# Flamingo block on one core: cross keys turned in a score bank, weight means one step sooner, another order for the step without a tile

## The chip, the cores and the metric

One core of a Trainium2 chip runs the whole kernel. The metric is device time in microseconds (us), median of repeated runs. The engines are TensorE (PE; its weight loads PEld), VectorE (DVE), ScalarE (ACT), GpSimd (POOL) and SyncE (SP), which issues most transfers. Each works through its own list of instructions in order and waits only at semaphores.

## What is computed

```python
x = x + tanh(g_xattn) * xattn(layernorm(x), ctx)      # x: 8 x 112 x 512, ctx: 8 x 375 x 512
x = x + tanh(g_ffn) * moe_ffn(layernorm(x))           # 8 experts, top 2

# xattn: 16 query heads, 8 key/value heads of 128
q  = ln(fp8_linear(h, wq));  k = ln(fp8_linear(h, wk));  v = fp8_linear(h, wv)
qx = ln(fp8_linear(h, wqx)); kx, vx = split(ctx @ w_kv_x.T); kx = ln(kx)
cat = concat(softmax(q k / sqrt(128)) v, softmax(qx kx / sqrt(128)) vx)
out = fp8_roundtrip(cat / smooth) @ wproj.T
```

## The kernel before

Four stages follow each other: the inputs are normalised and rounded, then attention, the output projection, and the experts. The change touches the attention alone.

**Steps.** The 16 query heads fall into four groups `g` of four, the batch has eight sequences `u`. A step takes a pair: `s = (g, u)`, whose projections are computed, and `t`, the one before it, whose attention is computed. So the two halves of a step are independent, and the engines interleave them. The 896 token rows make seven tiles of 128, though each sequence has 112 rows: steps 0 to 6 of a group have a tile of q, qx and k to project, **step 7 has none** and projects only values and the context (`has_tile`, `last_step`). `passes` writes steps 1 to 7 and 0 of the next group as the body of a loop run three times (groups 0 to 2), and those of group 3 once more without a loop. Time follows `u`: step 1 is the first of a body, and the step 0 that ends it does the first projections of the next group.

**Within a step.** On TensorE `project` 0 to 5 make q, qx, k with v, and three chunks of the context, each in a bank of `p_proj` in turn. `turn` 0 to 4 transpose the normalised q, qx, k and the two heads of the context keys (`nkx`) of `t` in the banks of `p_tr`, one after the other (0, 1, 0, 1, 0). `score_self` and `score_cross` 0 to 3 fill `p_self` and the two banks of `p_cross`; `turn_self` and `turn_cross` 0 to 3 transpose the probabilities in `p_tr`; `outputs` 0 and 1 multiply them with the values in `p_out`. `bank_free` holds the waits for the banks.

ScalarE takes projections out of PSUM and squares them (`take`), copies turned heads (`turned`), and makes the exponentials. VectorE sums the squares (`sums`), GpSimd makes `rs` of them (`rstd`), VectorE scales (`scale`). VectorE also finds the maxima, normalises the probabilities (`norm_self`, `norm_cross`), copies their transposes (`take_self`, `take_cross`), multiplies the output (`smoothed`), rounds it in five operations (`rounded`) and copies the next inputs (`inputs`). The order on every engine is written out by hand in its `step` and `last_step`.

Projections run in fp32 as sums of products of parts: weights and context are split into `hi` (ScalarE: `w_high`, `c_high`) and `lo` (VectorE: `w_low`; GpSimd: `c_low`). `c_low` of a chunk stands ahead of `rstd` of the same number in `last_step` on GpSimd: `c_low` 1, `rstd` 3, `c_low` 2, `rstd` 4, `rstd` 5.

**Weights of the next group.** 4 MB are fetched in step 1. For each of four blocks `k`, `weights.means` (L139, L142) sums the columns of each head on VectorE, and `weights.centre` (L158 to L163) subtracts the mean on ScalarE in three parts: in steps 2 to 5. `w_high` and `w_low` for queries (`change == "queries"`) stand in step 6, for keys and values (`"keys"`) in step 7, for the rest (`"new"`) in step 0.

## Time and profile before

| | us |
|---|---|
| three runs | 1277.56, 1278.98, 1281.84 (median 1278.98) |
| the profiled execution | 1275.52 |
| its span, first to last instruction | 1273.8 |
| TensorE busy, matmuls | 1120.3 (88%) |
| VectorE busy | 845.5 (66%) |
| ScalarE busy | 704.5 (55%) |
| GpSimd busy | 476.2 (37%) |
| granted TensorE clock, mean share of full speed | 0.951 |

The attention takes about the first 900 us of the span. In rows in order of time, the first number is the start and the second the duration in us; a bracket at the end holds how long the engine stood idle ahead of the row and which instruction ended that. A matmul's duration overlaps with the next one's; their pace is read from the starts.

### The profile page before, as it was taken

How to read it: one execution, taken by the hardware profiler on the slowest of the kernel's cores; microseconds unless marked ns; L12 is line 12 of the kernel's file. 1: busy time of each engine (PE TensorE's matmuls, PEld its weight loads, DVE VectorE, ACT ScalarE, POOL GpSimd, SP SyncE). 2: the span in 40 equal slices, each digit the busy share in tenths (PEclk: the TensorE clock that was granted, in tenths of full speed). 3: DMA queues.
4: the chain of work that ended last, by engine and by line, in shares of the span. 5: the costliest groups of instructions: out<-in, count | busy, mean ns of one | idle time of the engine just before them, and what ended most of it. 6: DMA issues, size and time to landing. Idle time of an engine off the chain costs nothing. (4 is left out here: it accounts for less than half of the span.)

```text
span 1273.8 us, 21650 instructions
## 1 busy us (share of the span) xinstructions
PE 1120.3 (88%) x5656; PEld 904.7 (71%) x5656; DVE 845.5 (66%) x1704; ACT 704.5 (55%) x1794; POOL 476.2 (37%) x584
## 2 busy tenths in 40 slices
PE   1099999899999979999988999997799949999996
PEld 1078777677777857877776788885588737777785
DVE  7967777786778768788777877876543665746100
ACT  7966777654777844676765646654111413434442
POOL 3074435343454423443443434432000132655432
PEclk9589999999999989999989999999899958999999
DMA  5041111114111111411111311110446066666220
GB/s 191 23 168 47 32 33 48 40 41 166 38 51 40 33 32 34 180 49 33 33 51 35 133 32 48 41 40 15 150 155 240 25 228 201 190 202 183 55 42 1
DMA packets 51736, 107.61 MB, mean 84 GB/s; under 512 B 5984, under 2 KB 26464, under 8 KB 49568
## 3 DMA queue, kind: packets, MB, share of 16 engines
q1 hardware_dynamic: 46912, 97.00, 23.2%
q0 software_dynamic: 4704, 9.18, 3.2%
q8 instruction: 55, 0.90, 0.3%
q14 instruction: 65, 0.53, 0.1%
HBM read 91.48 MB, written 16.52 MB: 85 GB/s over the span
## 5 line engine op out<-in xcount | busy, mean ns | idle before, releaser
L604 POOL TENSOR_TENSOR c_lo<-c_raw,c_hi 128x500 fp32r<-128x500 f32 x96 | 135.5, 1412 | 189.9 <-ACT c_hi L655 189.8
L806 PE MATMUL p_proj<-w_hi,xqs 128*128 128x512 f32 (+2 forms) x464 | 159.1, 362 | 51.2 <-DVE w_lo L529 41.0
L833 PE MATMUL p_proj<-w_hi,c_hi 128*125 128x512 f32 x384 | 167.9, 437 | 0.0
L591 POOL TENSOR_TENSOR va<-ss,epst 125x2 f32<-125x2 f32 (+1 forms) x180 | 61.6, 342 | 263.5 <-DVE ss L1000 263.5
L598 POOL TENSOR_TENSOR rs<-va,mhalf 125x2 f32<-125x2 f32 (+1 forms) x180 | 148.4, 825 | 15.6 <-POOL va L591 2.9
L833 PE MATMUL p_proj<-w_lo,c_hi 128*125 128x512 f32 x384 | 153.8, 401 | 0.0
L833 PE MATMUL p_proj<-w_hi,c_lo 128*125 128x512 f32 x384 | 153.7, 400 | 0.0
L806 PE MATMUL p_proj<-w_lo,xqs 128*128 128x512 f32 (+2 forms) x464 | 149.3, 341 | 0.0
L1000 DVE TENSOR_REDUCE ss<-sq 125x2 f32<-125x256 f32 (+1 forms) x180 | 89.7, 499 | 82.4 <-ACT sq L665 76.1
L806 PEld LDWEIGHTS p_proj<-w_hi,xqs 128*128 128x128 f32 (+1 forms) x464 | 87.2, 188 | 66.3 <-issue 45.0
L726 ACT ACTIVATE pcross<-p_cross,nmax 112x375 f32<-112x375 f32 x128 | 73.2, 577 | 78.2 <-DVE nmax L1029 77.3
L874 PE MATMUL p_cross<-kxT,qxT 128*112 128x375 f32 x256 | 97.4, 482 | 0.0
L1284 PE MATMUL p_acc<-p_hi,p_catr 128*128 128x512 f32 x224 | 88.5, 395 | 9.1 <-DVE p_lo L1329 9.1
L806 PEld LDWEIGHTS p_proj<-w_lo,xqs 128*128 128x128 f32 (+1 forms) x464 | 87.5, 189 | 8.5
L1284 PE MATMUL p_acc<-p_lo,p_catr 128*128 128x512 f32 x224 | 88.1, 393 | 0.0
L833 PEld LDWEIGHTS p_proj<-w_hi,c_hi 128*125 128x125 f32 x384 | 73.1, 190 | 20.0 <-issue 1.7
L158 ACT ACTIVATE shared<-shared,w_mean,wsc 128x128 f32<-128x128 f32 x160 | 65.9, 486 | 37.3 <-DVE w_mean L142 37.3
L833 PEld LDWEIGHTS p_proj<-w_hi,c_lo 128*125 128x125 f32 x384 | 72.7, 189 | 18.5
L833 PEld LDWEIGHTS p_proj<-w_lo,c_hi 128*125 128x125 f32 x384 | 73.0, 190 | 17.9 <-issue 0.3
L665 ACT ACTIVATE sq<-p_proj 125x256 f32<-125x256 f32 (+1 forms) x180 | 84.7, 470 | 0.0
L901 PE MATMUL p_out<-pcrossT,valx 125*128 125x224 f32 x384 | 84.3, 356 | 0.0
L1052 DVE TENSOR_TENSOR yb<-p_out,smg 128x448 bf16<-128x448 f32 x64 | 39.7, 621 | 61.8 <-PE p_out L901 61.8
(234 smaller groups left out, 2726.7 us busy)
## 6 DMA issues: line engine op xcount, KB each, us to landing
c_raw<-in_ctxT SPq DMA_DIRECT2D x96, 250.0 KB, 2.6
shared<-in_w_in SPq DMA_DIRECT2D x16, 1024.0 KB, 9.5
shared<-in_wproj SPq DMA_DIRECT2D x32, 256.0 KB, 2.8
raw_g<-in_Wg SPq DMA_DIRECT2D x8, 1024.0 KB, 6.7
raw_u<-in_Wu SPq DMA_DIRECT2D x8, 1024.0 KB, 5.9
raw_d<-in_Wd SPq DMA_DIRECT2D x8, 1024.0 KB, 5.5
cat_scratch<-cat SPq DMA_DIRECT2D x32, 224.0 KB, 2.0
shared<-cat_scratch SPq DMA_DIRECT2D x2, 1792.0 KB, 8.4
```

The costliest lines, as they stand in the source:

```text
L158: act.activation(cols, cols, ACT.Identity, bias=mean, scale=self.wsc[:, n, block_k])
L591: pool.tensor_tensor(va[0:rows, lo:hi], ss[0:rows, lo:hi], epst[0:rows, lo:hi], ALU.add).then_inc(va_done, 1)
L598: pool.tensor_tensor(rs[0:rows, lo:hi], va[0:rows, lo:hi], mhalf[0:rows, lo:hi], ALU.pow).then_inc(rs_done, 1)
L604: pool.tensor_tensor(flat(c_lo[:, k, :, :]), flat(c_raw[:, k, :, :]), flat(c_hi[:, k, :, :]).bitcast(F32), ALU.subtract).then_inc(cl_done, 1)
L665: act.activation(sq[0:rows, j % 2, 0:n], p_proj[0:rows, j % 2, 0:n], ACT.Square, scale=float(HD) ** -0.5).then_inc(pj_done, 1)
L726: act.activation(pcross[0:T, h, :], p_cross[0:T, h % 2, 0:TC], ACT.Exp, bias=nmax[0:T, 4 + h:5 + h], accum_out=lsum[0:T, 4 + h:5 + h]).the ...
L806: m = pe.matmul(out, xqs[:, n, k, 0:rows], (w_hi, w_lo)[i % 2][:, k, lo:lo + w], start=(i == 0), stop=(i == 2 * KB - 1))
L833: m = pe.matmul(bank[0:CT, :], a[:, ch, k, :], w[:, k, CKX:CV], start=(i == 0), stop=(i == 3 * KB - 1))
L874: pe.matmul(p_cross[0:T, h % 2, 0:TC], qxT[:, t[1] % 2, h, :], kxT[:, h // HPG, :], start=True, stop=True).then_inc(sx_rdy, 1)
L901: m = pe.matmul(p_out[:, HPG * T:2 * HPG * T], valx[0:CT, par, k, g * P:(g + 1) * P], flat(pcrossT[0:CT, k, HPG * g:HPG * (g + 1), :]), st ...
L1000: v.tensor_reduce(ss[0:rows, lo:hi], sq[0:rows, j % 2, 0:(hi - lo) * HD].rearrange("p (h d) -> p h d", d=HD), AX, ALU.add).then_inc(rd_don ...
L1284: m = pe.matmul(acc[:, j, :], catr[:, n % 2, j * P:(j + 1) * P], w[:, n % 2, :], start=(first and part == 0), stop=(last and part == 1), s ...
```

## The change

1. `turn_bank`: the first head of the context keys is turned in bank 1 of `p_cross`, the second in bank 1 of `p_tr`. The transposes of the probabilities change banks in turn; the waits of `bank_free` follow.
2. `means` of block `k` moves from step `k + 2`, ahead of `sums` 3, to step `k + 1`, behind `sums` 5. `centre` stays in steps 2 to 5, its third part ahead of `take` 5 instead of behind. `take` 3 comes ahead of `exp_cross` 2 and 3 on ScalarE.
3. `inputs` moves behind `norm_cross` 2 and 3.
4. `w_low` of the queries moves behind `scale` 5; `w_high` of the keys moves from step 6 to step 7.
5. `last_step` gets another order on TensorE, ScalarE and VectorE.

```diff
@@ -524,6 +524,10 @@
+    def turn_bank(n):
+        return p_cross[:, 1, :] if n == 3 else p_tr[:, {0: 0, 1: 1, 2: 0, 4: 1}[n], :]
     def split_low(eng, n):
@@ -699,11 +703,11 @@
             if n >= 3:
-                act.activation(kxT[:, n - 3, :], p_tr[:, n % 2, 0:TC], ACT.Identity, bias=b,
+                act.activation(kxT[:, n - 3, :], turn_bank(n)[:, 0:TC], ACT.Identity, bias=b,
                                scale=w).then_inc(t_done, 1)
...
             heads = (4, 4, 2)[n]
-            src = p_tr[:, n % 2, 0:heads * P].rearrange("p (h t) -> p h t", t=P)
+            src = turn_bank(n)[:, 0:heads * P].rearrange("p (h t) -> p h t", t=P)
             dst, u = (qT, qxT, kT)[n], t[1]
@@ -732,8 +736,9 @@
             turned(t, 2)
+            c_high(s, 1)
+            if change == "keys": w_high(g, 2, change)
             turned(t, 3)
-            c_high(s, 1)
             take(s, 3)
@@ -766,17 +771,16 @@
             if A: c_high(s, 2)
+            if A: take(s, 3)
             if Q: exp_cross(t, 2)
             if Q: exp_cross(t, 3)
-            if A: take(s, 3)
             if k is not None: weights.centre(act, g, k, 0)
...
             if k is not None: weights.centre(act, g, k, 1)
+            if k is not None: weights.centre(act, g, k, 2)
             if change == "queries": w_high(g, 1, change)
             if A: take(s, 5)
-            if k is not None: weights.centre(act, g, k, 2)
-            if change == "queries": w_high(g, 2, change)
             if A and s[1] == TJ - 1: c_high((s[0], B - 1), 0)
@@ -837,13 +841,15 @@
             if n < 2:
-                pe.wait_ge(pt_done, 5 * lin(t) + 4 + n)
-            elif n < 5 and not has_tile(t):
-                pe.wait_ge(pt_done, 5 * lin(t) + 4 + n % 2)
-            elif n < 7:
-                pe.wait_ge(t_done, td_no(t, n - 2))
+                pe.wait_ge(pt_done, 5 * lin(t) + 5 - n)
+            elif n == 3:
+                pe.wait_ge(ex_done, 4 * lin(t) + 4)
+            elif n >= 7:
+                pe.wait_ge(pt_done, 5 * (lin(t) + 1) + n - 6)
+            elif n < 6 and not has_tile(t):
+                pe.wait_ge(pt_done, 5 * lin(t) + n)
             else:
-                pe.wait_ge(pt_done, 5 * (lin(t) + 1) + n - 6)
+                pe.wait_ge(t_done, td_no(t, {2: 0, 4: 1, 5: 2, 6: 4}[n]))
@@ -852,10 +858,10 @@
                 for h in range((4, 4, 2)[n]):
-                    m = pe.transpose(p_tr[:, n % 2, h * P:(h + 1) * P], src[:, h * P:(h + 1) * P], ident[:, :])
+                    m = pe.transpose(turn_bank(n)[:, h * P:(h + 1) * P], src[:, h * P:(h + 1) * P], ident[:, :])
             else:
                 for k in range(NC):
-                    m = pe.transpose(p_tr[:, n % 2, k * CT:(k + 1) * CT],
+                    m = pe.transpose(turn_bank(n)[:, k * CT:(k + 1) * CT],
                                      nkx[0:CT, k, (n - 3) * P:(n - 2) * P], ident[0:CT, 0:CT])
@@ -878,14 +884,14 @@
             for h in range(HP):
-                m = pe.transpose(p_tr[0:T, 1, h * T:(h + 1) * T], pself[0:T, h, :], ident[0:T, 0:T])
+                m = pe.transpose(p_tr[0:T, 0, h * T:(h + 1) * T], pself[0:T, h, :], ident[0:T, 0:T])
             m.then_inc(tr_rdy, 1)
...
             for k in range(NC):
-                m = pe.transpose(p_tr[0:CT, h % 2, k * T:(k + 1) * T], pcross[0:T, h, k * CT:(k + 1) * CT],
+                m = pe.transpose(p_tr[0:CT, 1 - h % 2, k * T:(k + 1) * T], pcross[0:T, h, k * CT:(k + 1) * CT],
                                  ident[0:T, 0:T])
@@ -909,8 +915,8 @@
             turn(t, 2)
+            project(s, 3)
             turn(t, 3)
-            project(s, 3)
             score_self(t)
@@ -922,9 +928,9 @@
             project(s, 5)
-            outputs(t, 0)
             turn_cross(t, 2)
             turn_cross(t, 3)
+            outputs(t, 0)
             outputs(t, 1)
@@ -1039,13 +1045,13 @@
             v.wait_ge(ou_rdy, 2 * lin(t) + 2)
-            v.tensor_copy(flat(pselfT[0:T, :, :]), p_tr[0:T, 1, 0:HP * T]).then_inc(pt_done, 1)
+            v.tensor_copy(flat(pselfT[0:T, :, :]), p_tr[0:T, 0, 0:HP * T]).then_inc(pt_done, 1)
...
             v.tensor_copy(pcrossT[0:CT, :, h, :],
-                          p_tr[0:CT, h % 2, 0:NC * T].rearrange("p (k t) -> p k t", k=NC)).then_inc(pt_done, 1)
+                          p_tr[0:CT, 1 - h % 2, 0:NC * T].rearrange("p (k t) -> p k t", k=NC)).then_inc(pt_done, 1)
@@ -1072,31 +1078,31 @@
             if change == "keys": w_low(g, 1)
-            sums(s, 3)
             max_self(t)
-            scale(s, 3)
             max_cross(t, 0)
...
             norm_cross(t, 1)
+            sums(s, 3)
             take_self(t)
-            sums(s, 4)
             take_cross(t, 0)
             max_cross(t, 2)
-            scale(s, 4)
+            scale(s, 3)
             take_cross(t, 1)
             max_cross(t, 3)
-            if change == "keys": inputs((s[0] + 1, 0))
+            sums(s, 4)
             norm_cross(t, 2)
             norm_cross(t, 3)
-            if change == "keys": w_low(g, 2)
-            smoothed(t, 0)
+            if change == "keys": inputs((s[0] + 1, 0))
+            scale(s, 4)
             take_cross(t, 2)
             take_cross(t, 3)
+            smoothed(t, 0)
             sums(s, 5)
...
             scale(s, 5)
+            if change == "keys": w_low(g, 2)
             rounded(t)
@@ -1123,10 +1129,9 @@
             if A: scale(s, 2)
-            if A: inputs((s[0], s[1] + 1))
             if Q: norm_cross(t, 2)
             if Q: norm_cross(t, 3)
-            if k is not None: weights.means(v, g, k)
+            if A: inputs((s[0], s[1] + 1))
             if A: sums(s, 3)
@@ -1135,9 +1140,10 @@
             if A: scale(s, 4)
+            if A: sums(s, 5)
+            if change is None and g is not None and s[1] <= KB: weights.means(v, g, s[1] - 1)
+            if A: scale(s, 5)
             if change == "queries": w_low(g, 0)
-            if A: sums(s, 5)
-            if A: scale(s, 5)
             if Q: rounded(t)
```

VectorE in a centring step, before: step 2 of a group (`w_mean` is the tile of means, `shared` the weights, `ss` the sums of squares).

```order
L1036 TENSOR_SCALAR pcross<-pcross,linv 112x375
L136 ISA
L137 ISA
L139 TENSOR_REDUCE w_mean<-shared 128x12
L142 TENSOR_TENSOR w_mean<-w_mean,wmul 128x12
L995 REGISTER_ALU
L1000 TENSOR_REDUCE ss<-sq 125x2
L1051 ISA
L1052 TENSOR_TENSOR yb<-p_out,smg 128x448
L1045 REGISTER_ALU
L1047 COPY pcrossT<-p_tr 125x3x112
```

The same in the change, where it stands in step 1.

```order
L1006 TENSOR_REDUCE ss<-sq 125x2
L136 ISA
L137 ISA
L139 TENSOR_REDUCE w_mean<-shared 128x12
L142 TENSOR_TENSOR w_mean<-w_mean,wmul 128x12
L1012 REGISTER_ALU
L1015 TENSOR_TENSOR nkx<-nkx,rs 125x256
L1066 TENSOR_SCALAR yb<-yb 128x896
```

The two operations on `w_mean` leave the place ahead of the third chunk's sum and `pcrossT`, and stand between the last `ss` and the last scaling of `nkx`.

VectorE at the end of step 6 and the start of step 7, before (`w_lo` 128x4x512 is the queries' part, `yb` the output being rounded).

```order
L1052 TENSOR_TENSOR yb<-p_out,smg 128x448
L1006 REGISTER_ALU
L1009 TENSOR_TENSOR nkx<-nkx,rs 125x256
L529 TENSOR_TENSOR w_lo<-shared,w_hi 128x4x512
L995 REGISTER_ALU
L1000 TENSOR_REDUCE ss<-sq 125x2
L1006 REGISTER_ALU
L1009 TENSOR_TENSOR nkx<-nkx,rs 125x256
L1060 TENSOR_SCALAR yb<-yb 128x896
```

And in the change.

```order
L1058 TENSOR_TENSOR yb<-p_out,smg 128x448
L1012 REGISTER_ALU
L1015 TENSOR_TENSOR nkx<-nkx,rs 125x256
L1001 REGISTER_ALU
L1006 TENSOR_REDUCE ss<-sq 125x2
L1012 REGISTER_ALU
L1015 TENSOR_TENSOR nkx<-nkx,rs 125x256
L533 TENSOR_TENSOR w_lo<-shared,w_hi 128x4x512
L1066 TENSOR_SCALAR yb<-yb 128x896
```

`ss` and `nkx` of the last chunk change places with `w_lo`.

TensorE at the end of step 7, behind project 5, before.

```order
L898 MATMUL p_out<-pselfT,val 128x224
L901 MATMUL p_out<-pcrossT,valx 128x224 x3
L885 REGISTER_ALU
L846 REGISTER_ALU
L888 MATMUL p_tr<-ident,pcross 125x112 x3
L885 REGISTER_ALU
L888 MATMUL p_tr<-ident,pcross 125x112 x3
L895 REGISTER_ALU
L897 REGISTER_ALU
L898 MATMUL p_out<-pselfT,val 128x224
```

And in the change.

```order
L894 MATMUL p_tr<-ident,pcross 125x112 x3
L891 REGISTER_ALU
L848 REGISTER_ALU
L894 MATMUL p_tr<-ident,pcross 125x112 x3
L903 REGISTER_ALU
L904 MATMUL p_out<-pselfT,val 128x224
L907 MATMUL p_out<-pcrossT,valx 128x224 x3
L901 REGISTER_ALU
L903 REGISTER_ALU
L904 MATMUL p_out<-pselfT,val 128x224
```

Both transposes of `pcross` stand ahead of both `outputs` (`p_out`) now.

## Rows read from the trace of the kernel before

**Rows 1.** TensorE in order of time: turn 0 at the steps' starts (start us, us, engine, line, operation)
```profile
235.42 0.60 PE L855 MATMUL p_tr<-ident,nq 128*128 128x128 f32 x4
...
294.00 0.60 PE L855 MATMUL p_tr<-ident,nq 128*128 128x128 f32 x4
...
319.69 0.49 PE L855 MATMUL p_tr<-ident,nq 128*128 128x128 f32 x3
...
444.71 0.60 PE L855 MATMUL p_tr<-ident,nq 128*128 128x128 f32 x4
...
506.70 0.60 PE L855 MATMUL p_tr<-ident,nq 128*128 128x128 f32 x4
...
656.75 0.60 PE L855 MATMUL p_tr<-ident,nq 128*128 128x128 f32 x4
...
715.26 0.60 PE L855 MATMUL p_tr<-ident,nq 128*128 128x128 f32 x4
...
739.67 0.60 PE L855 MATMUL p_tr<-ident,nq 128*128 128x128 f32 x4
...
859.81 0.60 PE L855 MATMUL p_tr<-ident,nq 128*128 128x128 f32 x4
```

**Rows 2.** In order of time: waits in the centring steps 4 and 5 of group 1
```profile
374.35 0.38 PE L806 MATMUL p_proj<-w_hi,xqs 128*128 128x256 f32 x1 [0.43 <-ACT sq L665]
...
414.55 1.75 DVE L139 TENSOR_REDUCE w_mean<-shared 128x12 f32<-128x1536 f32 x1
...
416.62 1.65 ACT L158 ACTIVATE shared<-shared,w_mean,wsc 128x128 f32<-128x128 f32 x4 [3.10 <-DVE w_mean L142]
...
418.42 0.64 PE L898 MATMUL p_out<-pselfT,val 112*128 112x224 f32 x2 [0.34 <-DVE pcrossT L1047]
```

**Rows 3.** TensorE in order of time: step 7 of group 1
```profile
451.07 0.88 PE L858 MATMUL p_tr<-ident,nkx 125*128 125x125 f32 x3 [3.88 <-DVE nkx L1009]
...
456.82 0.95 PE L867 MATMUL p_self<-kT,qT 128*112 128x112 f32 x8
...
464.00 0.60 PE L881 MATMUL p_tr<-ident,pself 112*112 112x112 f32 x4 [1.87 <-DVE pself L1023]
...
474.78 1.11 PE L898 MATMUL p_out<-pselfT,val 112*128 112x224 f32 x2 [1.99 <-DVE pcrossT L1047]
```

**Rows 4.** Step 7 by stretch: us, busy PE, PEld, DVE, ACT, POOL, clock, DMA share, GB/s
```profile
451.00:453.00 2.00, 1.93 (x6) 1.68 (x7) 1.77 (x5) 1.01 (x2) 0.00 (x0) 0.50 0.00 0
```

**Rows 5.** In order of time: ends of step 7, and step 0, groups 1 and 2
```profile
472.07 1.22 DVE L529 TENSOR_TENSOR w_lo<-shared,w_hi 128x1024 fp32r<-128x1024 f32 x1
...
491.03 0.60 PE L881 MATMUL p_tr<-ident,pself 112*112 112x112 f32 x4 [0.59 <-DVE pself L1023]
...
688.08 0.56 PE L806 MATMUL p_proj<-w_hi,xqs 128*128 128x512 f32 x1
...
701.02 0.59 PE L881 MATMUL p_tr<-ident,pself 112*112 112x112 f32 x4 [1.26 <-DVE pself L1023]
```

**Rows 6.** In order of time: keys scaled and turned in group 3
```profile
813.64 0.42 DVE L1009 TENSOR_TENSOR nkx<-nkx,rs 125x256 f32<-125x256 f32 x1 [1.08 <-POOL rs L598]
...
815.89 0.48 PE L858 MATMUL p_tr<-ident,nkx 125*128 125x125 f32 x3
```

**Rows 7.** VectorE in order of time: step 7 of group 1
```profile
445.79 2.28 DVE L529 TENSOR_TENSOR w_lo<-shared,w_hi 128x2048 fp32r<-128x2048 f32 x1
...
449.48 1.45 DVE L1009 TENSOR_TENSOR nkx<-nkx,rs 125x256 f32<-125x256 f32 x1 [1.08 <-POOL rs L598]
...
453.43 3.34 DVE L529 TENSOR_TENSOR w_lo<-shared,w_hi 128x2048 fp32r<-128x2048 f32 x1
...
460.70 0.61 DVE L1015 TENSOR_REDUCE nmax<-p_self 112x4 f32<-112x448 f32 x1
```

**Rows 8.** GpSimd in order of time: step 7 of group 1
```profile
449.42 1.24 POOL L604 TENSOR_TENSOR c_lo<-c_raw,c_hi 128x500 fp32r<-128x500 f32 x1
```

**Rows 9.** TensorE in order of time: step 7 of group 3
```profile
874.29 0.59 PE L881 MATMUL p_tr<-ident,pself 112*112 112x112 f32 x4 [1.92 <-DVE pself L1023]
```

## The prediction

> **What bounds the kernel now.** I read the TensorE rows of the attention in order of time first, since the transposes of the query heads (turn 0) mark every step 1 to 7 of a group. From turn 0 of step 2 to turn 0 of step 7, five periods, it takes 125.0 us in group 1, and 120.1 us in group 3, where no weights are centred [rows 1]. (The last period is some 2 us short, as step 7 has no project 0.) So 4.9 us per group hang on the centring, 14.6 us in three groups. From turn 0 of step 7 to turn 0 of the next step 1 (step 7 and step 0) it takes 58.6, 62.0 and 58.5 us [rows 1]. TensorE is the bound nearly everywhere else in the attention: it waits only where a row shows a bracket.
>
> In a centring step two short waits stand on TensorE: project 2 waits 0.43 us for ScalarE's squares, and the second `outputs` waits 0.34 us for `pcrossT` [rows 2]. Both have one source. VectorE's sum over the weight tile (1.75 us) stands ahead of the copies of `pcrossT`, and ScalarE's centring waits 3.10 us for it, so ScalarE is late into the next step [rows 2]. Records of pipelined matmuls hide part of such waits, which is why I price them by the periods.
>
> In step 7 TensorE stands still 3.88 us ahead of turn 3, runs then at a granted clock of 0.50 (the 1.2 GHz level) and reaches the self scores only at 456.82; it waits 1.87 us for `pself` and 1.99 us for `pcrossT` [rows 3, 4]. Step 0 adds 0.59 us in group 1 and 1.26 us in group 2 [rows 5].
>
> **Means one step sooner, centring ahead of take 5.** The operations and their sizes stay; 12 sums of 1.75 us, each with a multiplication, move behind `sums` 5 and ahead of `scale` 5. Removed: the 2.0 us ahead of the `pcrossT` copies, and ScalarE's 3.10 us wait, since the means are a step old. The first two centring parts (1.65 us each) fit into the stretch in which ScalarE waited 3.10 us [rows 2], and the third comes ahead of take 5 instead of ahead of the next step's turns. If every step came down to group 3's, this would be the whole 14.6 us. Added: 2.0 us ahead of `scale` 5, where VectorE waits 1.08 us for `rs` anyway; so the keys are scaled 0.9 us later. In group 3 they are ready at 814.06 and turn 3 starts at 815.89, 1.8 us later [rows 6]. 0.9 us of cover is left, so I cost it at nothing. The sum now also reads the weights at the end of step 1; they are asked for at the step's start, and whether they have landed in time is a small rival. Bounds: 14.6 us, and below, if half of the waits stay, 7.3 us. I take **14 us**.
>
> **Keys turned in a score bank.** `kx` head 0 goes to `p_cross` bank 1, where it waits for the last exponentials of the step before, long done; head 1 goes to bank 1 of `p_tr`. No row shows TensorE waiting for these banks, so the edit by itself is worth nothing. Inputs behind the cross normalisation: 1.5 us of casts change place with work that TensorE needs only after project 5. Nothing either, in ordinary steps. Nor for `take` 3 ahead of the last two cross exponentials: project 3 is done by then, and ScalarE waits there for VectorE's maxima; its cover gone, it would delay the exponentials by the take's own length, which only the transposes behind project 4 would feel.
>
> **Step 7, group 1, followed through.** Before, `w_lo` of the queries (2.28 us) stood ahead of `sums` 5 [rows 7]. Now the sum follows `scale` 4 directly. That brings everything behind it 2.2 us forward: POOL's `c_lo` of chunk 0 from 449.42 to 447.2, done 448.5 [rows 8]. TensorE does project 3 ahead of turn 3 now. It is free at 447.2 (3.88 us before 451.07) and waits 1.3 us for `c_lo`. Project 3 took 5.2 us at half the clock [rows 3, 4], so 2.6 at least at full clock; with the weight loads I take 2.9. Turn 3 adds 0.4, the self scores start at 451.8 instead of 456.82: 5.0 us sooner.
>
> But VectorE isn't there yet. `scale` 5 runs beside `c_lo` as before (1.45 us) and ends at 448.7. Behind it stand `w_lo` of the queries, the rounding (450.93 to 453.43, 2.5 us) and the next `w_lo`, 2.28 us each alone, 3.34 us beside a `c_lo` [rows 7]. With one of each this ends at 448.7 + 3.34 + 2.6 + 2.28 = 456.9. Only then comes the maximum of the self scores, which started at 460.70 [rows 7]. `sums` 3 and `scale` 3 are out of this chain, so `pself` is turned 3.2 us after it: 460.1 instead of 464.00, 3.9 us sooner. TensorE's work from the self scores to there is 5.3 us (456.82 to 464.00 less 1.87), so it is free at 457.1 and waits 3.0 us. **The stall moves from the scaled keys to VectorE's `w_lo` chain.** With 2.28 us for both `w_lo` it would be 2.0 us.
>
> Here the two orders of VectorE and POOL matter. `scale` 5 started 0.06 us behind a `c_lo` of 1.24 us and took 1.45 us instead of the 0.42 of group 3; the second `w_lo` took 3.34 us and not 2.28 [rows 6 to 8]. The Trainium skill ("SBUF — State Buffer", Who interferes with whom) says that such a pair takes turns at one port pair and that the later one blocks until the first is done. By that rule `w_lo`, which starts at 448.7 right before `c_lo` of chunk 1, would keep its 2.28 us and POOL would pay, and the forecast would be 3 us lower.
>
> From `pself` on: `sums` 3 stands behind the second cross normalisation, 1.0 us after `pself` is turned. POOL needs its statistics (0.9 us) ahead of `c_lo` of chunk 2 (1.25 us), so project 5 can start 3.6 us after `pself` is turned. Project 5 takes 2.9, the last two cross transposes 0.8, `outputs` 0 1.45. Then `outputs` 1 must wait for `smoothed` 0, since both use `p_out`: 0.65 us, new. After 1.45 us more project 0 starts: 10.85 us after `pself` is turned. In group 1 `outputs` 1 alone began 10.8 us after it (464.00 to 474.78) [rows 3]. `w_lo` of the keys (1.22 us) is out of this stretch [rows 5], and stands ahead of the rounding now: step 0's VectorE chain, on which TensorE waited, is 1.2 us longer. From project 0 to the next `pself` it was 12.9 us in group 2 (688.08 to 701.02) [rows 5]; now 12.95 + 1.2 = 14.15.
>
> The sum from turn 0 of step 7 to the next `pself`: 15.4 + 10.85 + 14.15 = 40.4 us, 121.2 in three groups. From there to turn 0 of step 1 nothing changes: 14.2 us in group 2 (701.02 to 715.26) and 15.7 in group 1 (491.03 to 506.70), which I take for group 0 too: 45.6 [rows 1, 5]. That makes 166.8, against 58.6 + 62.0 + 58.5 = 179.1: 12.3 us less. A wait of 3.88 us brought half clock [rows 3, 4]; the new one of 3.0 us may too. It cost 2.6 us at project 3; here part of it lies under POOL's late `c_lo`, so up to 2 us per group: 6.3 us is the lower bound. With two short `w_lo` each group is 1 us sooner: 15.3 us is the upper. I take **10 us**, below the middle, since the new wait is nearer to the one of 3.88 us.
>
> In group 3 there is no `w_lo`, so `pself` is ready for TensorE when it comes: turn 0 at 859.81, `c_lo` at +3.75 as before, project 3 to +6.65, and 5.3 + 0.4 us of work: +12.4 instead of +14.48 [rows 1, 9]. The rest is as above. **2.2 us.** The last step without a projection keeps its order.
>
> **Sum.** 14 + 10 + 2.2 = 26.2 us. The profiled execution took 1275.5 us, 3.5 below the median of 1279.0 that the forecast is for. 1279.0 − 26.2 = **1253 us**. Everything behind the attention starts sooner by the same amount.
>
> **Rivals.**
> *The last step returns nothing:* half clock after the new 3.0 us wait, project 5 behind POOL, and the longer chain of step 0 take back what project 3 gains. For it: three new waits on one path. Against: project 3 no longer stands behind a 3.88 us stall. 1279 − 16 = 1263. Chance 0.12.
> *Centring doesn't pay:* ScalarE stays late, because centring part 2 ahead of take 5 delays the squares of projection 5. Against it: its wait of 3.10 us is given back ahead of them [rows 2]. 1279 − 12 = 1267. Chance 0.05.
> *Both return nothing, stalls only change names:* 1279. Chance 0.03.
> *Slower:* the means ahead of `scale` 5 hold up turn 3. Place: the end of steps 1 to 4, 12 times. It begins to cost beyond the 0.9 us of cover. Up to 2.1 us beyond that it only eats the 26 us that the rest brings, and from there the kernel is slower. At 2 us it may also bring half clock, some 2.6 us each time as at project 3: 12 × 4.6 = 55 us, so 1253 + 55 = 1308. It needs a `scale` 5 that is 2.9 us later than now rather than 0.9, as through weights that haven't landed. Chance 0.04.
>
> **Numbers.** Forecast 0.76 at 1253, with its own range of 1245 to 1259 (the two bounds of step 7, and 1 us of each other term). The range reaches down to 1244 for the port rule and to 1264 to take in the first rival. Less than 0.3% (3.8 us) can't be told from no change: faster 0.93, same 0.03, slower 0.04.
>
> **What would show it.** Right: the five periods of turn 0 near 120.5 us in groups 0 to 2; no wait of ScalarE for the means; self scores of step 7 some 7.1 us after its turn 0; a wait for `pself` of 2 to 3 us in step 7 of groups 0 to 2 and none in group 3; a longer wait than 0.59 us in step 0. Wrong: TensorE waiting for `nkx` in steps 2 to 5, the five periods still at 125 us, or a long stretch at clock 0.50 in the second half of step 7.

## The result: 1247.7 us, 31.7 us less

| | before | after |
|---|---|---|
| median of four runs, us | 1279.34 (1277.56 to 1281.84) | 1247.68 (1244.3 to 1250.32) |
| the profiled execution | 1275.52 | 1250.32 |
| its span | 1273.8 | 1248.6 |

The ratio is 0.975, with a 95% interval of 0.9721 to 0.9779. The forecast was 1253 us, a sum of 26.2 us. The profiled execution of the changed kernel is the slowest of its four, and that of before lies below all four of its runs, so the two profiled times differ by 25.2 us and the medians by 31.7. Up to turn 0 of the last step 7 the traces differ by 30.5 us (859.81 against 829.28). What lies behind that took 414.0 us before and 419.3 after; a second execution of the kernel before, below, took 417.4 us there. Nearly all of it is the projection and the experts, whose code is the same. From the first matmul of the projection to the end the kernel before took 367.0 us with 49.5 us at half clock, its second execution 370.4 us with 56.4, and the changed kernel 371.3 us with 57.3. I compare the attention by traces, and whole kernels by medians.

The profile after, by busy time of the engines, from the page:

```profile
PE 1105.4 (89%) x5656; PEld 903.2 (72%) x5656; DVE 841.9 (67%) x1704; ACT 705.0 (56%) x1794; POOL 487.5 (39%) x584
```

Turn 0 at the steps' starts, TensorE in order of time, the changed kernel, groups 1 to 3 (line numbers behind the edit are 4 to 6 higher):

```profile
311.81 0.60 PE L861 MATMUL p_tr<-ident,nq 128*128 128x128 f32 x4
...
430.83 0.60 PE L861 MATMUL p_tr<-ident,nq 128*128 128x128 f32 x4
...
486.73 0.60 PE L861 MATMUL p_tr<-ident,nq 128*128 128x128 f32 x4
...
630.46 0.60 PE L861 MATMUL p_tr<-ident,nq 128*128 128x128 f32 x4
...
685.60 0.60 PE L861 MATMUL p_tr<-ident,nq 128*128 128x128 f32 x4
...
709.86 0.60 PE L861 MATMUL p_tr<-ident,nq 128*128 128x128 f32 x4
...
829.28 0.60 PE L861 MATMUL p_tr<-ident,nq 128*128 128x128 f32 x4
```

Against [rows 1], the five periods of group 1 fell from 125.0 to 119.0 us. That is 1.1 us below the 120.1 that I took for the floor, and group 3, which has no weights to centre, fell too: from 120.1 to 119.4. Steps 7 and 0 fell from 62.0 to 55.9 in group 1 and from 58.5 to 55.1 in group 2, but in group 0 only from 58.6 to 58.2.

The waits of [rows 2] are gone. Steps 4 and 5 of group 1, VectorE, ScalarE and TensorE in order of time; the sum over the weight tile runs behind `sums` 5 and ScalarE waits for none of it:

```profile
383.84 1.75 DVE L139 TENSOR_REDUCE w_mean<-shared 128x12 f32<-128x1536 f32 x1
...
400.29 1.64 ACT L158 ACTIVATE shared<-shared,w_mean,wsc 128x128 f32<-128x128 f32 x4
...
412.13 0.39 PE L810 MATMUL p_proj<-w_hi,xqs 128*128 128x256 f32 x1 [0.15 <-ACT sq L669]
```

Step 7 of group 1, TensorE, the answer to [rows 3, 5]:

```profile
434.72 0.47 PE L837 MATMUL p_proj<-w_hi,c_hi 128*125 128x512 f32 x1 [1.68 <-POOL c_lo L608]
...
437.91 0.95 PE L873 MATMUL p_self<-kT,qT 128*112 128x112 f32 x8
...
445.98 0.59 PE L887 MATMUL p_tr<-ident,pself 112*112 112x112 f32 x4 [2.46 <-DVE pself L1029]
...
449.70 0.47 PE L837 MATMUL p_proj<-w_hi,c_hi 128*125 128x512 f32 x1 [0.60 <-POOL c_lo L608]
...
455.65 0.65 PE L904 MATMUL p_out<-pselfT,val 112*128 112x224 f32 x2 [0.72 <-DVE yb L1058]
...
457.11 0.56 PE L810 MATMUL p_proj<-w_hi,xqs 128*128 128x512 f32 x1
...
464.26 0.34 PE L810 MATMUL p_proj<-w_hi,xqs 128*112 128x256 f32 x1 [1.81 <-DVE w_lo L533]
...
471.55 0.60 PE L887 MATMUL p_tr<-ident,pself 112*112 112x112 f32 x4 [0.94 <-DVE pself L1029]
```

One stall of 3.88 us has become a chain of small ones: 1.68 for POOL's `c_lo`, 2.46 for VectorE's `pself`, then 0.60, 0.72, 1.81 and 0.94.

### The profile page after: what moved, and what is told of

The parts are those of the page before. It is cut to its first block and busy times, and to the rows that moved or that the text cites. A ratio compares the mean times of both kernels' runs of the same rounds, so it can differ in the third digit from the quotient of the medians.

```text
span 1248.6 us, 21647 instructions
## 1 busy us (share of the span) xinstructions
PE 1105.4 (89%) x5656; PEld 903.2 (72%) x5656; DVE 841.9 (67%) x1704; ACT 705.0 (56%) x1794; POOL 487.5 (39%) x584
## 5 line engine op out<-in xcount | busy, mean ns | idle before, releaser
L608 POOL TENSOR_TENSOR c_lo<-c_raw,c_hi 128x500 fp32r<-128x500 f32 x96 | 143.3, 1493 | 158.0 <-ACT c_hi L659 157.8
L602 POOL TENSOR_TENSOR rs<-va,mhalf 125x2 f32<-125x2 f32 (+1 forms) x180 | 154.6, 859 | 15.6 <-POOL va L595 2.9
L595 POOL TENSOR_TENSOR va<-ss,epst 125x2 f32<-125x2 f32 (+1 forms) x180 | 59.9, 333 | 251.8 <-DVE ss L1006 251.7
L810 PEld LDWEIGHTS p_proj<-w_hi,xqs 128*128 128x128 f32 (+1 forms) x464 | 86.7, 187 | 70.3 <-issue 52.6
L1006 DVE TENSOR_REDUCE ss<-sq 125x2 f32<-125x256 f32 (+1 forms) x180 | 89.3, 497 | 46.3 <-ACT sq L669 43.4
L730 ACT ACTIVATE pcross<-p_cross,nmax 112x375 f32<-112x375 f32 x128 | 73.2, 579 | 53.7 <-DVE nmax L1035 50.6
L880 PE MATMUL p_cross<-kxT,qxT 128*112 128x375 f32 x256 | 100.9, 497 | 0.1
L692 ACT ACTIVATE nkx<-p_proj 125x256 f32<-125x256 f32 x96 | 37.8, 394 | 73.3 <-PE p_proj L837 65.0
```

What stands on the lines that cost most here:

```text
L595: pool.tensor_tensor(va[0:rows, lo:hi], ss[0:rows, lo:hi], epst[0:rows, lo:hi], ALU.add).then_inc(va_done, 1)
L602: pool.tensor_tensor(rs[0:rows, lo:hi], va[0:rows, lo:hi], mhalf[0:rows, lo:hi], ALU.pow).then_inc(rs_done, 1)
L608: pool.tensor_tensor(flat(c_lo[:, k, :, :]), flat(c_raw[:, k, :, :]), flat(c_hi[:, k, :, :]).bitcast(F32), ALU.subtract).then_inc(cl_done, 1)
L730: act.activation(pcross[0:T, h, :], p_cross[0:T, h % 2, 0:TC], ACT.Exp, bias=nmax[0:T, 4 + h:5 + h], accum_out=lsum[0:T, 4 + h:5 + h]).the ...
L810: m = pe.matmul(out, xqs[:, n, k, 0:rows], (w_hi, w_lo)[i % 2][:, k, lo:lo + w], start=(i == 0), stop=(i == 2 * KB - 1))
L880: pe.matmul(p_cross[0:T, h % 2, 0:TC], qxT[:, t[1] % 2, h, :], kxT[:, h // HPG, :], start=True, stop=True).then_inc(sx_rdy, 1)
```

## The experiments

All kernels ran with their own runs of the kernel before (medians 1279.2, 1279.5 and 1278.2 us in the three sets). The last four columns are worked out from the traces. "Attention" goes from turn 0 of the first group's step 1 to turn 0 of the last group's step 7. "Half clock" is how long the granted clock stood at 0.50, the 1.2 GHz level, between turn 0 of step 7 and the next turn 0, from windows of 1 us.

| kernel | median, us | less than before | attention | five periods, g0 / g1 / g2 / g3 | steps 7 and 0, g0 / g1 / g2 | half clock there |
|---|---|---|---|---|---|---|
| before | 1279.3 | | 774.3 | 125.0 / 125.0 / 125.0 / 120.1 | 58.6 / 62.0 / 58.5 | 6.8 / 13.6 / 6.8 |
| e9 before again | 1277.9 | | 772.9 | 124.9 / 124.9 / 124.9 / 120.1 | 59.7 / 59.7 / 58.5 | 6.8 / 6.8 / 6.8 |
| changed | 1247.7 | 31.7 | 743.6 | 119.1 / 119.0 / 119.1 / 119.4 | 58.2 / 55.9 / 55.1 | 10.2 / 0 / 3.4 |
| e1 inputs | 1271.3 | 7.9 | 769.4 | 125.1 / 125.1 / 125.1 / 119.4 | 59.9 / 58.8 / 58.0 | 6.8 / 3.4 / 6.8 |
| e2 means, centring | 1262.0 | 17.2 | 756.1 | 120.0 / 120.2 / 120.2 / 120.0 | 59.0 / 58.7 / 57.8 | 6.8 / 3.4 / 3.4 |
| e5 means alone | 1262.8 | 16.7 | 756.9 | 120.1 / 120.0 / 120.1 / 120.0 | 59.2 / 59.7 / 58.4 | 3.4 / 6.8 / 6.8 |
| e3 last step | 1268.2 | 11.0 | 763.3 | 124.9 / 124.9 / 124.9 / 120.1 | 56.9 / 56.9 / 55.1 | 3.4 / 6.8 / 3.4 |
| e4 banks as before | 1248.5 | 30.7 | 742.1 | 119.1 / 119.1 / 119.0 / 119.4 | 56.1 / 56.9 / 54.7 | 3.4 / 3.4 / 3.4 |
| e10 inputs as before | 1250.5 | 27.7 | 747.3 | 120.0 / 120.1 / 120.1 / 120.0 | 55.9 / 55.8 / 55.0 | 3.4 / 3.4 / 3.4 |
| e6 `c_low` | 1247.6 | 31.9 | 743.6 | 119.1 / 119.1 / 119.1 / 119.5 | 56.1 / 57.1 / 55.9 | 3.4 / 6.8 / 10.2 |
| e7 `w_low` | 1240.8 | 38.7 | 734.9 | 119.1 / 119.1 / 119.0 / 119.5 | 54.3 / 54.0 / 52.5 | 0 / 0 / 0 |
| e12 (e6 and e7) | 1237.9 | 40.3 | 733.9 | 119.1 / 119.1 / 119.1 / 119.4 | 53.7 / 53.6 / 52.6 | 0 / 0 / 3.4 |
| e8 (e12 and two more) | 1231.3 | 48.2 | 729.7 | 119.1 / 119.1 / 119.1 / 119.5 | 52.7 / 52.2 / 50.5 | 3.4 / 0 / 0 |
| e11 `w_low` 1 on POOL | 1237.0 | 41.2 | 736.6 | 119.0 / 119.1 / 119.1 / 119.4 | 55.0 / 54.4 / 53.1 | 3.4 / 3.4 / 3.4 |

### e2 and e5: the means

```diff
             if Q: norm_cross(t, 3)
-            if k is not None: weights.means(v, g, k)
...
             if A: sums(s, 5)
+            if change is None and g is not None and s[1] <= KB: weights.means(v, g, s[1] - 1)
```

e2 also has centring part 2 ahead of `take` 5; e5 is this edit alone.

> The kernel before, with the means one step sooner (behind sums 5 of steps 1 to 4) and the third centring part ahead of take 5; inputs, banks and the last step as before. My prediction: the five periods from turn 0 of step 2 to turn 0 of step 7 fall from 125.0 to 120.1 us, so 14 us less, 1265 us (bounds 7.3 and 14.6 less). The rival by which centring part 2 ahead of take 5 holds up ScalarE: no gain, periods at 125 us, 1279 us. The rival by which the means hold up scale 5: TensorE waits for nkx in steps 2 to 5, over 1279 us.

> The kernel before, with the means one step sooner and nothing else: the third centring part stays behind take 5. If the means ahead of the pcrossT copies were the whole cause of the 4.9 us per group, the periods fall to 120.1 us and the time by 14 us, to 1265 us. If the third centring part ahead of the next step's turns costs as much as ScalarE's lateness did, half of it stays: periods near 122.5 us, 1272 us. If the means ahead of scale 5 hold up turn 3, TensorE waits for nkx and the time is over 1279 us.

e2: ratio 0.9867 (0.9845 to 0.9888), 17.2 us less. e5: 0.9867 (0.985 to 0.9883), 16.7 us less. Turn 0 of steps 2 and 7 of group 1 in e2:

```profile
314.62 0.60 PE L855 MATMUL p_tr<-ident,nq 128*128 128x128 f32 x4
...
434.79 0.60 PE L855 MATMUL p_tr<-ident,nq 128*128 128x128 f32 x4
```

That is 120.2 us, and in three groups the five periods give back 14.7 us (375.1 less 360.4), the whole of the term. TensorE's waits for `pcrossT` are gone in steps 2 to 5, and its waits of 0.43 us at project 2 fell to 0.16 us at most, so the place of the sum ahead of these copies was the cause. The place of centring part 2 is worth nothing: e5, without it, has the same periods. The rival by which it costs something, and the one by which the means hold up turn 3, both fall.

### e1 and e10: the casts of the next inputs

```diff
-            if A: inputs((s[0], s[1] + 1))
             if Q: norm_cross(t, 2)
             if Q: norm_cross(t, 3)
+            if A: inputs((s[0], s[1] + 1))
```

e1 is this edit alone; e10 is the changed kernel without it.

> The kernel before, with one edit: in the steps with a tile the casts of the next inputs stand behind the normalisation of cross heads 2 and 3. My prediction costed this at nothing: 1279 us, ordinary steps of group 3 still 24.42 us apart. The other theory, from the trace of the changed kernel: the ordinary steps there are 24.16 to 24.26 us apart, because the last two normalised cross heads are ready sooner for their transposes. If this edit alone brings that, 0.17 us in each of some 28 steps is 5 us: 1274 us, and the transposes of cross heads 2 and 3 begin without their short stall.

> The changed kernel, with the casts of the next inputs ahead of the normalisation of cross heads 2 and 3 again. My prediction costed the move at nothing: 1248 us. By the other theory (with the casts ahead, the last normalised cross head comes 0.16 us late for its transposes in every step): the five periods go from 119.06 back to 120.1 us in all groups, step 1 loses another 0.5 us, and the time is 5 to 6 us longer, 1253 to 1254 us.

e1: 0.9939 (0.9918 to 0.996), 1271.3 us, 7.9 us less. e10: 0.9784 (0.9759 to 0.9808), 1250.5 us, 27.7 us less, against 31.7 for the changed kernel. The interval of e10 overlaps that of the changed kernel, so there the whole time doesn't settle it; e1's time and the rows do. I had costed the move at nothing, and that was wrong; the 1253 to 1254 us that my other theory gave for e10 was too much. TensorE's transposes of cross heads 2 and 3, in the kernel before, in an ordinary step of group 3 and in a centring step of group 1:

```profile
781.54 0.97 PE L888 MATMUL p_tr<-ident,pcross 112*125 112x112 f32 x6
...
362.60 1.02 PE L888 MATMUL p_tr<-ident,pcross 112*125 112x112 f32 x6
```

The same group 3 step in e1, and `outputs` 1 of a centring step of group 1 there:

```profile
777.70 0.81 PE L888 MATMUL p_tr<-ident,pcross 112*125 112x112 f32 x6
...
367.03 0.64 PE L898 MATMUL p_out<-pselfT,val 112*128 112x224 f32 x2 [0.62 <-DVE pcrossT L1047]
```

The six transposes took 0.94 to 1.03 us in steps 1 to 5 of every group before and take 0.81 in e1. No bracket stands at the longer rows: the wait lies inside the group, where the last three transposes need head 3. In the kernel before, VectorE began to normalise it at 781.46, behind the casts, while TensorE began at 781.54. Moving the casts takes some 0.15 to 0.2 us off each of steps 2 to 5 of group 3 (five periods of 119.4 us instead of 120.1). In the centring steps it gives e1 nothing, since the means still stood ahead of the copies: the `pcrossT` wait grew from 0.34 to 0.62 us. With the means gone it is worth 0.2 to 0.4 us in each of these steps as well, 120.1 to 119.1 over the five periods. So it needs the other edit to pay in full.

The traces of e10 and the changed kernel price it at 1.0 us in each of three groups, 0.6 in group 3 and 2.7 us from turn 0 of step 1 to that of step 2 (100.4 less 97.7 us over four groups): 6.3 us. In step 1 there is more than the wait in the transposes: in group 1 of e10 `pself` is turned 11.29 us behind turn 0, after a wait of 0.27 us for VectorE, and in the changed kernel at 10.86 without one. What makes VectorE late there I haven't traced, and the stretch differs between kernels whose casts stand as before (99.4 us in e5, 99.6 in e3), so 5.3 us is as well supported as 6.3. Over the whole attention e10 is 3.7 us longer than the changed kernel and 5.2 longer than e4, since steps 7 and 0, where executions differ, gave some back. In e1 the same places give only 0.6 and 2.1 us, 2.7 together. Its median says 7.9 less, at least 5.1 by the interval, and its nine runs go from 1268.0 to 1278.5; the difference isn't placed, and I take the price from e10's trace. The medians of e1, e2 and e3 add up to 36.1 us, the changed kernel gives 31.7; that is within what the four intervals allow together.

### e3: the last step

```diff
 # TensorE, last step
-            turn(t, 3)
             project(s, 3)
+            turn(t, 3)
...
-            outputs(t, 0)
             turn_cross(t, 2)
             turn_cross(t, 3)
+            outputs(t, 0)
```

The changed orders of ScalarE and VectorE go with it, as do `w_low` 0 behind `scale` 5 and `w_high` 2 in step 7.

> The kernel before, with the changed order of the last step on all engines, w_low 0 of the queries behind scale 5 and w_high 2 moved into step 7; banks, inputs of ordinary steps, means and centring as before. My prediction: 10 us less in steps 7 and 0 of groups 0 to 2 (bounds 6.3 and 15.3) and 2.2 us less in group 3, so 1267 us; self scores of step 7 some 7.1 us after its turn 0. The rival by which the last step returns nothing: 1279 us. From the trace of the changed kernel, where group 3's step came out 0.9 us longer and the others 9.8 us shorter: 1270 us.

0.9917 (0.9899 to 0.9936), 11.0 us less. Steps 7 and 0 of groups 0 to 2 add up to 168.9 us, against 179.1 and 177.9 in the two executions of the kernel before: 9 to 10.2 us, as forecast. Group 3 gives almost nothing, here too (below). The new orders of TensorE, ScalarE and VectorE were run only together, so what each of them is worth is not shown.

### e4: the banks

```diff
     def turn_bank(n):
-        return p_cross[:, 1, :] if n == 3 else p_tr[:, {0: 0, 1: 1, 2: 0, 4: 1}[n], :]
+        return p_tr[:, n % 2, :]
```

> The changed kernel, with the banks of the transposes and of the turned cross keys as in the kernel before, everything else as changed. My prediction costed the banks at nothing: the time of the changed kernel, 1248 us. The other theory: the banks alone free TensorE from short waits for the copies of the turned keys (the banks then alternate otherwise), and part of the 0.17 us per ordinary step is theirs: up to 5 us more, 1253 us.

0.9763 (0.9743 to 0.9782), 1248.5 us: the same as the changed kernel's 1247.7 within the intervals. The banks are worth nothing, as forecast.

### e9: the kernel before, once more

> The kernel before once more, unchanged, for a second profile. If the 61.99 us from turn 0 of step 7 to the next turn 0 in group 1 belong to the kernel (its order of work), they stand here again. If they come from how long the granted clock stayed at 0.50 in that execution (6.8 us at half clock early in step 7 and 6.8 us around step 0 there, 3.4 us each in group 0), the value is another, between 58 and 62 us, and the time at half clock with it, while the five periods stay at 125.0 and 120.1 us.

One run, 1277.89 us. Turn 0 of step 7 and of the next step 1 in group 1:

```profile
445.61 0.60 PE L855 MATMUL p_tr<-ident,nq 128*128 128x128 f32 x4
...
505.32 0.60 PE L855 MATMUL p_tr<-ident,nq 128*128 128x128 f32 x4
```

59.7 us, not 62.0. The stretch behind the step's `outputs`, in the first execution and in this one (us, busy PE, PEld, DVE, ACT, POOL, clock, DMA share, GB/s):

```profile
474.00:480.00 6.00, 5.22 (x13) 4.54 (x14) 2.74 (x8) 0.00 (x0) 0.89 (x2) 0.50 0.00 0
```

```profile
475.00:481.00 6.00, 6.00 (x22) 5.01 (x22) 4.03 (x8) 1.04 (x3) 0.89 (x2) 0.72 0.00 0
```

The 61.99 us that I took as a base for group 1 held 6.8 us at half clock more than this execution does, half of it here and half early in step 7. 2.3 us of it were never the kernel's (1.1 us over the three groups, since group 0 came out longer here).

### e6, e7 and e12: which of the small stalls is on the path

```diff
 # e6, GpSimd: c_low of step 7 sooner
                 for j in range(3, 6):
+                    if j == 5 and s[1] == TJ - 1:
+                        c_low((s[0], B - 1), 0)
                     rstd(s, j)
-                if s[1] == TJ - 1:
-                    c_low((s[0], B - 1), 0)
 # e7, VectorE, step 6
             if A: sums(s, 4)
+            if change == "queries": w_low(g, 0)
             if Q: smoothed(t, 1)
...
             if A: scale(s, 5)
-            if change == "queries": w_low(g, 0)
```

e12 has both.

> The changed kernel, with POOL's c_low of chunk 0 for step 7 ahead of the last rstd of step 6. Project 3 of step 7 waits 1.68 us for it in each of four groups. If that wait is on the path, the kernel is up to 6.7 us faster than the changed one, 1241 us, and the self scores of step 7 come 5.4 us after its turn 0 instead of 7.1. If the time is only passed on to the wait for pself (2.46 us in groups 0 to 2, set by VectorE's chain), nothing is gained there and 1.7 us at most in group 3: 1246 us. If the last rstd, now 1.3 us later, delays scale 5 and so the whole of VectorE's chain, it is slower, 1252 us.

> The changed kernel, with w_low 0 of the queries (2.28 us) between sums 4 and smoothed 1 of step 6, where VectorE stands idle 2.8 us, instead of behind scale 5. If VectorE's chain behind scale 5 sets the wait for pself (2.46 us) in step 7 of groups 0 to 2, the wait goes: some 2.3 us per group, with the half clock that follows it in groups 0 and 2 up to 3.5 us, so 7 to 10 us less than the changed kernel, 1238 to 1241 us. If the stall only changes its name (project 4 or 5 then waits for POOL), 1248 us. If w_low in the gap holds up scale 4 and c_low, slower, 1252 us.

> The changed kernel with two of the edits together: w_low 0 of the queries in VectorE's idle time of step 6 (alone 7.8 us less than the changed kernel) and c_low of chunk 0 ahead of the last rstd of step 6 (alone 0 to 1 us). If c_low alone gained nothing only because the wait for pself grew by as much, it gains its full 1.68 us in four groups here: 1234 us, self scores 5.4 us after turn 0 in step 7 and pself 1.7 us sooner than 13.1. If project 3's wait never was on the path: 1241 us, as with w_low in the idle time alone.

Against the kernel before: e6 0.9744 (0.973 to 0.9758), e7 0.9693 (0.968 to 0.9706), e12 0.9681 (0.9656 to 0.9707). The self scores and the next `pself` of group 1's step 7 in e6, whose turn 0 is at 430.05:

```profile
435.34 0.95 PE L873 MATMUL p_self<-kT,qT 128*112 128x112 f32 x8
...
444.82 0.99 PE L887 MATMUL p_tr<-ident,pself 112*112 112x112 f32 x4 [3.85 <-DVE pself L1029]
```

The same in e7, whose turn 0 is at 427.81:

```profile
434.89 0.95 PE L873 MATMUL p_self<-kT,qT 128*112 128x112 f32 x8
...
440.95 0.60 PE L887 MATMUL p_tr<-ident,pself 112*112 112x112 f32 x4 [0.42 <-DVE pself L1029]
```

And in e12, turn 0 at 426.22:

```profile
431.52 0.95 PE L873 MATMUL p_self<-kT,qT 128*112 128x112 f32 x8
...
438.77 0.59 PE L887 MATMUL p_tr<-ident,pself 112*112 112x112 f32 x4 [1.63 <-DVE pself L1029]
```

e6 removes the wait of 1.68 us, the scores come 1.8 us sooner (+5.3), and `pself` waits 3.85 us instead of 2.46: VectorE's chain sets the path, the gain is 0.4 us at that point and none that the time shows. In group 3, where no `w_lo` stands in that chain, the gain is kept: `pself` is turned 11.3 us behind turn 0 instead of 13.1, and the projection stage begins at +46.3 instead of +48.0 us. e7 shortens that chain by its 2.28 us: `pself` at +13.1 instead of +15.1, no half clock in steps 7 and 0, and 6.9 us less than the changed kernel. With both, `pself` comes at +12.55, 0.6 us sooner than in e7 and not 1.7: VectorE is the bound again. e12's median is 2.9 us below e7's, but its ratio to its own runs of before is the same within the interval, so the time doesn't resolve what `c_low` adds; in the traces the attention up to the last step 7 is 1.0 us shorter (733.9 against 734.9) and the projection stage begins 2.1 us sooner behind it (+46.1 against +48.3). My expectation of 1234 us was too low.

### e8 and e11: further down the same chain

e8 adds to e12 that POOL does `c_low` of chunk 2 ahead of `rstd` 3, and that VectorE does `w_low` 2 of the keys ahead of `smoothed` 1. e11 hands VectorE's `w_low` 1 to POOL:

```diff
 # e8, GpSimd and VectorE, last step
                 c_low(s, 1)
-                rstd(s, 3)
                 c_low(s, 2)
+                rstd(s, 3)
...
             sums(s, 5)
+            if change == "keys": w_low(g, 2)
             smoothed(t, 1)
             scale(s, 5)
-            if change == "keys": w_low(g, 2)
 # e11, on top of e8
                 c_low(s, 1)
+                if change == "keys": w_low(g, 1)
                 c_low(s, 2)
...
-            if change == "keys": w_low(g, 1)
             max_self(t)
```

> The changed kernel, with c_low of chunk 0 sooner, c_low of chunk 2 ahead of rstd 3 in the last step, w_low 0 in VectorE's idle time of step 6 and w_low 2 of the keys ahead of smoothed 1. If the waits at project 3 (1.68 us), pself (2.46 us) and in step 0 (0.65 to 1.8 us) are all on the path and nothing takes their place: 12 to 15 us less than the changed kernel, 1233 to 1236 us. If VectorE and POOL only share their port the other way, with no stall removed: 1248 us.

> The kernel with w_low 0 in the gap, w_low 2 and both c_low sooner (1231 us), with w_low 1 of the queries taken from the head of VectorE's last step to POOL, behind its c_low of chunk 1, where POOL stood idle over 8 us. If VectorE's 2.28 us ahead of the maximum of the self scores are what the last wait for pself in step 7 (1.65 us in groups 0 to 2) hangs on: the wait goes, 1.65 us in three groups and half clock that follows it at times, 5 to 7 us, so 1225 us. If POOL, with 5.1 us for 2048 columns (1.25 us for 500 by its c_lo rows), holds up VectorE's operations beside it, or chunk 2 comes late for project 5: no gain or slower, 1231 to 1236 us.

e8: 0.9626 (0.9611 to 0.964), 1231.3 us, 16.4 us less than the changed kernel; **it beats both the kernel before and the changed one**, and my expectation of 1233 to 1236 us. The waits for `c_lo` at projects 3 and 5 and for the keys' `w_lo` in step 0 are gone. Left in group 1 are 1.67 us for `pself` and 0.98 for `smoothed` in step 7, and 1.23 for `pself` in step 0. The two further edits were not run apart.

e11: 0.968 (0.9657 to 0.9704), 1237.0 us, 5.7 us slower than e8 and 1 us above the range that I had given for a hold-up. POOL and VectorE in step 7 of group 1:

```profile
433.15 4.71 POOL L533 TENSOR_TENSOR w_lo<-shared,w_hi 128x2048 fp32r<-128x2048 f32 x1
...
433.47 4.87 DVE L1074 TENSOR_TENSOR ysum<-yb,ye 128x896 bf16<-128x896 bf16 x1
...
442.17 0.60 PE L888 MATMUL p_tr<-ident,pself 112*112 112x112 f32 x4 [3.64 <-DVE pself L1030]
```

VectorE's addition takes 0.62 us when it runs alone (e8). Here it began 0.32 us behind POOL's subtraction and took 4.87 us, to 0.5 us behind POOL's end. The 2.28 us that were taken from VectorE came back as 4.25 us of blocking: `pself` waited 3.64 us and was turned 14.56 us behind turn 0, against 12.56 in e8. 3.4 us at half clock followed in each of groups 0 to 2.

## Why the prediction was right, point by point

**Means and centring, 14 us: right.** 14.7 us in e2, and the mechanism was as I had it. The third centring part, which I moved with it in thought, has no share.

**Inputs, nothing: wrong, and the largest miss.** The step reads that the casts "change place with work that TensorE needs only after project 5". But the transposes of cross heads 2 and 3 stand ahead of project 5, and TensorE needs the heads at that moment: head 3 came 0.13 to 0.2 us late in steps 1 to 5 of every group and in the step 0 behind groups 0 to 2. The move is worth 5.3 to 6.3 us by the traces, and 3 to 8 by the medians of e10 and e1. The floor of 120.1 us, read off group 3, held this wait too. It stood in the trace of before: the same six transposes take 0.81 us in step 6 of group 1 (at 439.79), where only one of the four casts stands ahead of them, and 1.02 in step 5. This term is as large as the whole 5.5 us by which the forecast is off; the two wrong terms, this one and group 3, have opposite signs, and so the total came out nearer than they did.

**Steps 7 and 0 of groups 0 to 2, 10 us: right, at 9.8 us by the two traces and 9 to 10.2 by e3.** That it meets 10 so nearly is partly luck: with the same last step e4 has 167.7 us there and e10 166.7, so the gain is 8.7 to 12.4 us by the executions that are compared. In the changed kernel's trace group 0 gives 0.3 us of it, group 1 6.1 and group 2 3.4. Group 1 step by step:

| stretch | forecast, us | measured |
|---|---|---|
| turn 0 to the self scores | 7.1 | 7.08 |
| wait at project 3 for `c_lo` | 1.3 | 1.68 |
| turn 0 to `pself` | 15.4 | 15.15 |
| wait for `pself` | 3.0 (2.0 with two short `w_lo`) | 2.46 |
| `pself` to project 0 | 10.85 | 11.13 |
| project 0 to the next `pself` | 14.15 | 14.44 |
| from there to turn 0 | 15.7 | 15.18 |
| sum | 56.1 | 55.90 |

The stall did move to VectorE's `w_lo` chain, and e7, which cuts that chain and gains 6.9 us, shows that the chain sets it. Not foreseen: project 2 of step 0 waits 1.8 us for the keys' `w_lo`, which the new order puts behind `scale` 5. I had counted its 1.2 us in VectorE's chain for `pself` alone.

**Group 3, 2.2 us: wrong.** TensorE in its step 7, turn 0 at 829.28:

```profile
842.40 0.60 PE L887 MATMUL p_tr<-ident,pself 112*112 112x112 f32 x4 [0.50 <-DVE pself L1029]
...
846.13 0.47 PE L837 MATMUL p_proj<-w_hi,c_hi 128*125 128x512 f32 x1 [0.54 <-POOL c_lo L608]
...
852.10 0.62 PE L904 MATMUL p_out<-pselfT,val 112*128 112x224 f32 x2 [0.81 <-DVE yb L1058]
```

`pself` comes at +13.1, 1.4 us sooner than in [rows 9] and not 2.1, mostly since it still waits 0.50 us, which I had at nothing. Then project 5 waits for POOL's `c_lo` and `outputs` 1 for `smoothed`. The second `outputs` of that step, before:

```profile
882.96 0.65 PE L898 MATMUL p_out<-pselfT,val 112*128 112x224 f32 x2 [0.90 <-DVE pcrossT L1047]
```

From `pself` to this row it was 8.7 us before (874.29 to 882.96) and is 9.7 now (842.40 to 852.10). In group 1 the same stretch fell from 10.8 to 9.7 us (445.98 to 455.65). The projection stage began at +46.7 us in e3 and e10 and at +47.0 in both executions of before: 0.3 us. In the changed kernel's own trace, and in e4's, 3.4 us at half clock some 32 us behind turn 0, in the step behind it, made it +47.9 to +48.0. "The rest is as above" was the step that failed: the new order behind `pself` takes 9.7 us in either group. The other groups gain by it because the next group's casts and the keys' `w_lo` stood in that stretch before; in group 3 they never did, and the order costs 1 us there.

**The port pair: the rule was right and my sum wrong.** VectorE and POOL in step 7 of group 1, the answer to [rows 7, 8]:

```profile
434.78 2.28 DVE L533 TENSOR_TENSOR w_lo<-shared,w_hi 128x2048 fp32r<-128x2048 f32 x1
...
435.04 3.14 POOL L608 TENSOR_TENSOR c_lo<-c_raw,c_hi 128x500 fp32r<-128x500 f32 x1 [0.46 <-ACT c_hi L659]
...
440.62 2.28 DVE L533 TENSOR_TENSOR w_lo<-shared,w_hi 128x2048 fp32r<-128x2048 f32 x1
...
442.82 0.62 DVE L1021 TENSOR_REDUCE nmax<-p_self 112x4 f32<-112x448 f32 x1
```

`w_lo` began first and kept its 2.28 us; POOL's subtraction took 3.14 us instead of 1.24. I had charged 3.34 us to `w_lo`. The Trainium skill ("SBUF — State Buffer", Who interferes with whom) has the one that issues first keep the pair for its whole instruction; this trace agrees: POOL's subtraction, begun 0.26 us behind `w_lo`, ended 1.12 us behind it. e11 shows the other direction, with VectorE held up until POOL's 4.71 us were over.

**Half clock, up to 2 us per group: right in kind.** Against the sums that I had before any half clock (56.1, 56.1 and 54.6 us), groups 0 to 2 took 2.1 us more, 0.2 less and 0.5 more, with 10.2, 0 and 3.4 us at half clock. In step 7 it came in groups 0 and 2 and not in group 1:

```profile
247.00:249.00 2.00, 2.00 (x7) 1.25 (x5) 1.30 (x3) 1.01 (x4) 0.91 (x1) 0.50 0.11 6
...
447.00:449.00 2.00, 2.00 (x10) 0.97 (x9) 2.00 (x5) 2.00 (x6) 1.54 (x3) 1.00 0.03 8
...
647.00:649.00 2.00, 2.00 (x7) 1.33 (x6) 1.55 (x4) 1.61 (x4) 1.92 (x3) 0.50 0.03 8
```

**The banks, and `take` 3 ahead of the exponentials, nothing:** the first is shown by e4. The second was never run by itself; with the casts as before and the means moved, the five periods are 120.0 to 120.2 us both with it (e10) and without (e2), which leaves it no more than 0.1 us in five periods.

**The rivals.** "The last step returns nothing" falls to e3, "centring doesn't pay" to e2, the slower one to the traces: TensorE never waits for `nkx` in steps 2 to 5 of the changed kernel, and VectorE begins its sum over the weights in step 1 without an idle bracket, so they had landed.

## What to carry to other kernels

Where a group of like matmuls has different durations at different places of a program and the granted clock is the same, look for a wait inside the longer one, though no bracket says so; here a fifth of a microsecond in each of 23 steps was the largest part of this forecast's largest miss. Before a stall is removed, look at which engine's chain ends next: `c_low` alone moved 1.7 us from one wait to another in groups 0 to 2, while 2.3 us off VectorE's chain gained 7 us in three groups. Work handed to an idle engine isn't free when it holds up its neighbour: in e11 an addition of 0.62 us on VectorE, begun 0.32 us behind POOL's subtraction, took 4.87 us.

## What the runs showed of the hardware that was not expected

Whether TensorE's clock falls to its lower level behind a wait differs by group and by execution, for one and the same wait. Counted over these traces in step 7 of groups 0 to 2, half clock followed the stall of 3.6 to 3.9 us (for `nkx` or `pself`) in 21 of 21 cases, the wait for `pself` of 2.46 us in 7 of 12, of 1.5 to 1.7 us in 2 of 6, and of 0.42 us in none of 3. It began between 2.0 us before the end of the wait and 2.1 us behind it, and lasted 3.4 us or 6.8 us each time. Where the wait of 2.46 us brought none, in 4 of 5 cases 3.4 us came in step 0 instead. So e7, with the wait for `pself` 2.0 us shorter, gained 1.9 us in group 1, where the changed kernel had no half clock, and 3.9 and 2.6 us in groups 0 and 2, where it had. Two executions of the kernel before differ by 2.3 us in one group, with 13.6 and 6.8 us at half clock. A base taken from one execution carries that.

POOL's subtraction isn't in proportion to its size: 1.24 us for 500 columns, 4.71 us for 2048, where I had estimated 5.1 in proportion.
